# Who issues the fetches of the experts' first-layer weights in the routed FFN of a gated cross-attention block

## The chip, the cores and the metric

The kernel runs on one core of one Trainium2 chip. The metric is the device time of one execution in microseconds (us). The kernel before takes 317.39 us, the median of three runs (316.21 to 318.24).

## The reference, cut to what matters

4096 tokens (8 x 512) of width 256, float32. First a gated cross-attention, in which the 16 channels of a token's heads attend to one another, then a mixture of experts with top-1 routing:

```python
x = x + tanh(g_xattn[0]) * xattn(layernorm(x), ctx, Wq, Wk, Wv, Wo)
# ffn on xf = layernorm(x).reshape(4096, 256), E = 8 experts
idx = argmax(softmax(xf @ Wg + bg), axis=-1)
h   = gelu(einsum('th,ehi->tei', xf, W1) + b1)          # W1: 8 x 256 x 256
y   = einsum('tei,eih->teh', h, W2) + b2                # W2: 8 x 256 x 256
x   = x + tanh(g_ffn[0]) * take_along_axis(y, idx)      # one expert a token
```

## The kernel before, in words

**Two stages.** The first runs over 16 pairs of 128-token tiles: projections, scores, softmax, values, output projection, residual, gate logits. For each tile it works out each token's expert and its place, and scatters the rows (with mean, rstd and token number) to `routed_rows` in HBM, where each expert has a region. This stage ends at about 213 us of the trace.

**The expert stage** runs over 39 blocks (32 tiles + 8 experts - 1) of 128 routed rows, each block of one expert. Which rows and which expert a block has stands in the table `tab` in SBUF. So each fetch first loads an address or an expert number from `tab` into a register (`value_load`), then waits for its ring slot, then issues the DMA. Per block b, with ring slot q = b % 8 (`RING = 8`):

- SyncE (SP) fetches the block's rows, `xb[q]`, 134 KB, in `fetch` (L367 to L374). Before it may, it waits for `yf_done`, the end of block b - 8 on VectorE.
- The first-layer weights of the block's expert, `w1_sb[q]`, 257 KB, are fetched in `fetch_w1` (L315 to L319). SP does it for even q and for the first eight blocks. For odd q from block 9 on ScalarE does it (`act_fetches`, L321): in its slot b, behind the GELU of block b and the copy for block b + 2, it fetches w1 of block b + 3. Blocks 0 to 15 stand in the table's first part (`tab_done` 1), blocks 16 and up in its second (`tab_done` 2).
- VectorE normalizes (`norm_b`, L993): in its slot b the rows of block b + 3, and then it finishes block b - 1 (L1002, L1006, the last being `yf`).
- TensorE in its slot b does three things in a fixed order: layer 1 of block b (L557, 8 matmuls, waits for the copied transposes and for `w1_in[q]`), layer 2 of block b - 1 (L571, 4 matmuls), and the transposes of block b + 2 (L547, 2 matmuls). The order is written by hand.
- ScalarE in its slot b does the GELU of block b (L696), the copy of the transposes of block b + 2 (L703), and on even slots the fetch above.
- GpSimd stores the finished rows by an indirect DMA (L1244).

The second-layer weights of all experts stay in SBUF. Blocks 0 to 15 (`EARLY`) are written out one by one, with the end of the routing woven in; blocks 16 to 31 are two turns of a loop of eight blocks on each engine (`block_slots`, L268), with the block number in a register; blocks 32 to 38 are written out again. Each engine keeps its own order, and only semaphores tie them.

Of the kernel before, what the change touches and what calls it, by code (L numbers as in the profile page):

```python
# [32 lines left out]
RING = 8  # L33
OUT = 4
EARLY = 2 * RING
# [11 lines left out]
def wait(eng, sem, value):  # L47

    if isinstance(value, int) and value <= 0:
        return  # L50
    eng.wait_ge(sem, value)
# [27 lines left out]
def flamingo_block(nc, x, x_t, ctx_t, g_x, g_f, w_kv, w_qg, w_o, wo_t, bg, w1b, w2, b2, consts, out):  # L79
# [4 lines left out]
    blocks = tiles + E - 1  # L84
# [8 lines left out]
    with ExitStack() as stack:  # L93
# [6 lines left out]
        def sem(name):  # L100
            return stack.enter_context(nc.semaphore(name))
# [130 lines left out]
        tab_step, tab_done, turned = sem("tab_step"), sem("tab_done"), sem("turned")  # L232
# [34 lines left out]
        def block_slots(eng, slot, skew):  # L267
            with eng.Fori(EARLY // RING, blocks // RING) as turn:  # L268
                for q in range(RING):
                    slot(RING * turn + q, q, turn)  # L270
            for b in range(blocks - blocks % RING, blocks + skew):
                slot(b, b % RING, b // RING)
# [14 lines left out]
        def load_x(eng, n, i, count):  # L287
            wait(eng, x_in[i], count)
            eng.dma_start(x_sb[:, bass.ds(2 * n, 2), 0:D], x_v[:, bass.ds(2 * n, 2), :]).then_inc(x_in[i], 16)

        def load_ct(eng, n, i):
            wait(eng, kv_done, n - 1 if not isinstance(n, int) or n > 1 else 0)
            eng.dma_start(ct[i][:].rearrange("p a b c -> p (a b c)"),
                          ctx_t[bass.ds(n, 1)].rearrange("a p f -> p (a f)")).then_inc(ct_in[i], 16)

        def load_xt(eng, n, i):
            wait(eng, q_done, n - 1 if not isinstance(n, int) or n > 1 else 0)
            eng.dma_start(xt[i][:].rearrange("p a b c -> p (a b c)"),
                          x_t[bass.ds(n, 1)].rearrange("a p f -> p (a f)")).then_inc(xt_in[i], 16)

        def spread_k(eng, n, i, blocks_of):

            eng.wait_ge(yk_out, n + 1)
            for t in blocks_of:
                eng.dma_start(kb[i][H * t:H * t + H, t, :], y_k[i][H * t:H * t + H, :]).then_inc(kb_in[i], 16)

        def spread_v(eng, n, i, blocks_of):

            wait(eng, av_done, n - 1 if not isinstance(n, int) or n > 1 else 0)
            eng.wait_ge(yv_out, n + 1)  # L310
            for t in blocks_of:
                c, s = t // 2, t % 2
                eng.dma_start(vb[i][H * t:H * t + H, 4 * s + c, :], y_v[i][H * t:H * t + H, :]).then_inc(vb_in[i], 16)

        def fetch_w1(eng, b, q):  # L315

            ex = eng.value_load(tab[0:1, 1, bass.ds(b, 1)], min_val=0, max_val=E - 1)
            wait(eng, gelu_done, b - RING + 1)
            eng.dma_start(w1_sb[q][:], w1b[bass.ds(ex, 1)].rearrange("a p f -> p (a f)")).then_inc(w1_in[q], 16)  # L319

        def act_fetches(b, q):  # L321

            return q % 2 == 1 and not (isinstance(b, int) and b < RING)


        @block.sync
        def _(sp):
            def late_w2(e):
                sp.dma_start(w2_sb[:, bass.ds(e, 2)], w2[:, bass.ds(e, 2)]).then_inc(late_in, 16)

            def late_b2(e):
                sp.dma_start(b2_sb[:, bass.ds(e, 2), :].rearrange("p e d -> p (e d)"),
                             b2.rearrange("(e d) -> e d", d=D)[bass.ds(e, 2)].rearrange("e d -> (e d)").partition_broadcast(P)).then_inc(late_in, 16)
                sp.dma_start(rows.rearrange("(e r) w -> r e w", e=E)[0:P, bass.ds(e, 2)],
                             pad_row[:].unsqueeze(1).broadcast_to([P, 2, ROW])).then_inc(pad_in, 16)

            load_ct(sp, 0, 0)
            sp.dma_start(wkv[:, 1], w_kv[:, 1]).then_inc(wkv_in[1], 16)
            load_x(sp, 0, 0, 0)
            load_xt(sp, 0, 0)  # L340
            sp.dma_start(cst[:], consts).then_inc(cst_in, 16)
            load_xt(sp, 1, 1)
            sp.wait_ge(kb_clear[0], 1)
            spread_k(sp, 0, 0, range(4, T8))
            sp.wait_ge(vb_clear[0], 1)
            spread_v(sp, 0, 0, range(0, T8, 2))
            sp.wait_ge(kb_clear[1], 1)
            spread_k(sp, 1, 1, range(T8))
            sp.wait_ge(vb_clear[1], 1)
            spread_v(sp, 1, 1, range(T8))  # L350

            def slot(k, q):
                spread_k(sp, k + 2, q, range(T8))
                spread_v(sp, k + 2, q, range(T8))

            slot(0, 0)
            slot(1, 1)
            sp.wait_ge(consts_ok, 1)
            sp.wait_ge(wog_done, 1)
            with sp.Fori(1, E // 2 + 1) as turn:  # L360
                late_w2(2 * turn - 2)
                slot(2 * turn, 0)
                late_b2(2 * turn - 2)
                slot(2 * turn + 1, 1)
            for k in range(E + 2, pairs - 2):
                slot(k, k % 2)

            def fetch(b, q, turn):

                row = sp.value_load(tab[0:1, 0, bass.ds(b, 1)], min_val=0, max_val=(E - 1) * region + tokens)  # L370
                wait(sp, yf_done, b - RING + 1)
                sp.dma_start(xb[q][:], rows[bass.ds(row, P), :]).then_inc(xb_in[q], 16)
                if not act_fetches(b, q):
                    fetch_w1(sp, b, q)  # L374

            sp.wait_ge(tab_done, 1)
            sp.wait_ge(routed, 32 * (last_pair - 2))
            for b in range(EARLY):
                fetch(b, b % RING, b // RING)
            sp.wait_ge(tab_done, 2)  # L380
            sp.wait_ge(routed, 32 * pairs)
            sp.wait_ge(pad_in, 16 * E // 2)
            block_slots(sp, fetch, 0)
            for i in range(OUT):
                sp.wait_ge(stored[i], 16 * ((blocks + OUT - 1 - i) // OUT))
# [228 lines left out]
        def _(act):  # L614
# [64 lines left out]
            def expert_slot(b, q, turn):  # L679
                i = q % 2  # L680
                known = isinstance(b, int)
                if not known or b < blocks:
                    gelu(b, q)
                if not known or b + 2 < blocks:
                    copy_xbt(b + 2, i)
                ahead = 3
                if (not known or b + ahead < blocks) and act_fetches(b + ahead, (q + ahead) % RING):
                    fetch_w1(act, b + ahead, (q + ahead) % RING)

            def gelu(b, q):  # L690

                i = q % 2
                act.wait_ge(h_done, b + 1)
                wait(act, y_done, b - 1)
                for ic in range(KC):
                    last = act.activation(ht[i][:, ic, :], h_ps[i][:, ic * P:(ic + 1) * P], ACT.Gelu,  # L696
                                          bias=w1_sb[q][:, KC * D + ic:KC * D + ic + 1])
                last.then_inc(gelu_done, 1)

            def copy_xbt(b, i):  # L700
                act.wait_ge(xbt_done, b + 1)
                wait(act, h_done, b - 1)
                act.copy(xbt[i][:].rearrange("p a b -> p (a b)"), x_t_ps[i]).then_inc(xbt_out, 1)  # L703
# [5 lines left out]
            gelu(0, 0)  # L709
            copy_ot(last_pair)  # L710
            copy_xbt(2, 0)
            act.wait_ge(tab_done, 1)
            for b in range(1, EARLY):
                if b == EARLY - 3:
                    act.wait_ge(tab_done, 2)
                expert_slot(b, b % RING, b // RING)
            block_slots(act, expert_slot, 0)


# [591 lines left out]
```

## Time and profile before

| | us |
|---|---|
| median of 3 runs | 317.39 (316.21 to 318.24) |
| profiled execution, its own time | 320.28 |
| its span | 318.3 |
| TensorE busy | 287.7 (90%) |
| VectorE busy | 230.0 (72%) |
| ScalarE busy | 84.1 (26%) |
| GpSimd busy | 123.3 (39%) |
| mean granted TensorE clock | 0.982 |
| expert stage: layer 1 of block 1 to the last matmul | 220.9 to 308 |

The profiled execution took 2.9 us more than the median of the runs; 2.0 us of its time lie around its span. Issuing a DMA does not count as busy time, so SyncE has no line in the table; its issues stand in the timeline with their start and length. Matmuls of one engine overlap a little in the timeline, since their ends are modelled.

### The profile page before, as it was taken

To read this page: it belongs to the slowest core of one execution; us is meant where nothing else is said; L and a number is where in the kernel's file an instruction comes from. 1 tells how busy PE (TensorE), PEld (TensorE's weight loads), DVE (VectorE), ACT (ScalarE), POOL (GpSimd) and SP (SyncE) were. 2 spreads that over 40 slices of the span, in tenths; PEclk is the share of its full clock that TensorE was granted. 3 is DMA by queue.
4 is the path that set the end of the run, shared out by engine and by line. 5 is a ranking of instruction groups with operands and counts; after the bars stand their busy time and mean duration, and the time that the engine had idled before them with its cause. 6 is when DMAs were issued, how large, how long until landed. Compare 5 with 4: busy or idle time off the path is not lost.

```text
span 318.3 us, 10091 instructions
## 1 busy us (share of the span) xinstructions
PE 287.7 (90%) x3173; PEld 219.7 (69%) x3174; DVE 230.0 (72%) x810; ACT 84.1 (26%) x219; POOL 123.3 (39%) x125
## 2 busy tenths in 40 slices
PE   8989999999899999999999997687889998899870
PEld 7557767577577676776776775466778787889760
DVE  7558678797788888798887977867786664655550
ACT  1011320321312302303213213123434444454420
POOL 8502022442423523524424433432364444344441
PEclk9999999999999999999999999979999999999995
DMA  8575346466465565564455123277467887677610
GB/s 266 171 192 151 93 111 189 102 211 197 129 203 153 167 206 136 184 204 109 130 152 150 46 69 84 80 197 194 147 191 231 233 258 215 194 241 231 190 52 0
DMA packets 35482, 51.40 MB, mean 161 GB/s; under 512 B 8189, under 2 KB 18558, under 8 KB 35456
## 3 DMA queue, kind: packets, MB, share of 16 engines
q1 hardware_dynamic: 20240, 25.69, 30.7%
q10 hardware_dynamic: 11808, 16.81, 16.8%
q0 software_dynamic: 3408, 8.59, 7.6%
q8 instruction: 12, 0.20, 0.3%
q14 instruction: 14, 0.11, 0.1%
HBM read 32.99 MB, written 10.60 MB: 137 GB/s over the span
## 4 chain that ended last, share of the span: by engine, by line
PE 59%; issue 10%; DVE 10%; DMA 7%; ACTq 4%; POOL 3%; ACT 2%; another core or an unknown queue 1%; DVEq 1%; POOLq 0%
PE ps_pr L393 11%; PE ps_qo L401 11%; PE ps_av L439 5%; PE ps_tr L557 5%; PE ps_so L557 5%; PE ps_to L571 5%; PE ps_av L571 5%; PE ps_so L419 4%; DMA routed_rows<-sb_xs,sb_pos_i 4%; DMA sb_x<-x_in 3%; PE ps_pr L547 2%; POOL sb_cn L279 2%; PE ps_av L512 2%; PE ps_tr L428 1%; DVE sb_om L794 1%
## 5 line engine op out<-in xcount | busy, mean ns | idle before, releaser
L393 PE MATMUL ps_pr<-sb_wkv,sb_ct 128*128 128x512 f32 x128 | 63.0, 616 | 0.5 <-DVE sb_y_v L749 0.5
L279 POOL TENSOR_TENSOR sb_cn<-sb_om,sb_rt 128x512 f32<-128x512 f32 x15 | 19.3, 1287 | 68.5 <-DVE sb_om L794 68.5
L627 ACT ACTIVATE sb_pe_x<-sb_pe_x 128x512 f32<-128x512 f32 x16 | 10.1, 631 | 124.6 <-DVE sb_pe_x L770 108.2
L1213 POOL DMA_INDIRECT routed_rows<-sb_xs,sb_pos_i x32 | 32.2, 1006 | 21.0 <-DVE sb_pos_i L885 10.5
L393 PEld LDWEIGHTS ps_pr<-sb_wkv,sb_ct 128*128 128x128 f32 x128 | 22.3, 191 | 20.0 <-issue 19.8
L401 PE MATMUL ps_qo<-sb_wog,sb_ot 128*128 128x264 f32 x128 | 32.9, 402 | 1.3 <-ACT sb_q_n L622 1.1
L439 PE MATMUL ps_av<-sb_vb,sb_at 128*32 128x128 f32 x1024 | 32.6, 274 | 0.9 <-issue 0.9
L401 PEld LDWEIGHTS ps_qo<-sb_wog,sb_ot 128*128 128x128 f32 x128 | 25.2, 199 | 11.4 <-issue 7.3
L439 PEld LDWEIGHTS ps_av<-sb_vb,sb_at 128*32 128x32 f32 x1024 | 27.4, 110 | 7.1 <-issue 7.1
L419 PE MATMUL ps_so<-sb_kb,sb_y_q 128*32 128x128 f32 x1024 | 31.1, 273 | 0.5 <-DVE sb_y_q L755 0.5
L401 PE MATMUL ps_qo<-sb_wqg_c,sb_xt 128*128 128x264 f32 x128 | 31.1, 386 | 0.0
L1244 POOL DMA_INDIRECT out_rows<-sb_yf,sb_tok_i x20 | 19.7, 983 | 29.4 <-DVE sb_yf L1006 27.2
L419 PEld LDWEIGHTS ps_so<-sb_kb,sb_y_q 128*32 128x32 f32 x1024 | 28.0, 110 | 1.9 <-issue 1.4
L401 PEld LDWEIGHTS ps_qo<-sb_wqg_c,sb_xt 128*128 128x128 f32 x128 | 23.1, 190 | 3.6 <-DVE sb_wqg_c L1108 0.2
L1244 POOL DMA_INDIRECT out_rows<-sb_q_n,sb_tok_i x19 | 18.6, 980 | 17.2 <-issue 11.0
L557 PE MATMUL ps_tr<-sb_ct,sb_w 128*128 128x128 f32 x152 | 20.7, 279 | 4.1 <-ACT sb_ct L703 3.0
L1202 POOL TENSOR_TENSOR sb_rstd<-sb_ve,sb_neg_half 128x2 f32<-128x2 f32 x16 | 11.5, 716 | 33.1 <-ACT sb_q_n L622 18.2
L557 PEld LDWEIGHTS ps_tr<-sb_ct,sb_w 128*128 128x128 f32 x152 | 18.5, 191 | 5.8 <-ACT sb_ct L703 3.8
L1002 DVE TENSOR_TENSOR sb_yo<-ps_av,sb_b 128x256 f32<-128x256 f32 x20 | 8.5, 425 | 18.6 <-PE ps_av L571 12.5
L557 PE MATMUL ps_so<-sb_ct,sb_w 128*128 128x128 f32 x160 | 21.3, 276 | 0.1
L571 PE MATMUL ps_av<-sb_w,sb_ht 128*128 x80 | 21.3, 388 | 0.0
L571 PE MATMUL ps_to<-sb_w,sb_ht 128*128 x76 | 20.0, 385 | 1.3 <-ACT sb_ht L696 1.2
(129 smaller groups left out, 490.1 us busy)
## 6 DMA issues: line engine op xcount, KB each, us to landing
sb_w<-w_in_ SPq DMA_DIRECT2D x24, 257.0 KB, 3.2
sb_xb<-routed_rows SPq DMA_DIRECT2D x39, 134.0 KB
sb_kb<-sb_y_k SPq DMA_DIRECT2D x124, 32.0 KB
sb_vb<-sb_y_v SPq DMA_DIRECT2D x124, 32.0 KB
sb_w<-w_in_ ACTq DMA_DIRECT2D x15, 257.0 KB, 3.4
sb_ct<-ctx_in ACTq DMA_DIRECT2D x15, 256.0 KB, 3.2
sb_x<-x_in ACTq DMA_DIRECT2D x15, 256.0 KB, 5.6
sb_xt<-xt_in_ ACTq DMA_DIRECT2D x14, 256.0 KB, 4.1
```

The lines of the kernel that those rows point to most:

```text
L279: eng.tensor_tensor(cn[:].rearrange("p u h i -> p h u i"), om[:].rearrange("p h (u i) -> p h u i", u=2), rt[:].rearrange("p (u i) -> p u i ...
L393: last = pe.matmul(pr[:, s * 512:(s + 1) * 512], lhsT=ct[i][:, kc, s, :], rhs=wkv[:, kc, :], start=(kc == 0), stop=(kc == KC - 1))
L401: last = pe.matmul(dst[:, s * 512:s * 512 + DE], lhsT=src[:, kc, s, :], rhs=w[:, kc, :], start=(kc == 0), stop=(kc == KC - 1))
L419: last = pe.matmul(so[32 * q:32 * q + 32, r * P:(r + 1) * P], lhsT=y_q[:, 4 * q + r, u:u + 2, :].rearrange("p a b -> p (a b)"), rhs=kb[i][ ...
L439: last = pe.matmul(av[32 * q:32 * q + 32, r * P:(r + 1) * P], lhsT=at[:, 4 * r + q, u:u + 2, :].rearrange("p a b -> p (a b)"), rhs=vb[i][: ...
L557: last = pe.matmul(h_ps[i][:, ic * P:(ic + 1) * P], lhsT=w1_sb[q][:, kc * D + ic * P:kc * D + (ic + 1) * P], rhs=xbt[i][:, kc, :], start=( ...
L571: last = pe.matmul(y_ps[i], lhsT=ht[i][:, ic, :], rhs=w2_sb[:, bass.ds(ex, 1), ic, :].rearrange("p a d -> p (a d)"), start=(ic == 0), stop ...
L627: act.activation(pe_x[:], pe_x[:], ACT.Exp, scale=float(H) ** -0.5).then_inc(exp_done, 1)
L1002: dve.tensor_tensor(yo[i][:], y_ps[i], b2_sb[:, bass.ds(ex, 1), :].rearrange("p a d -> p (a d)"), ALU.add).then_inc(yb_done, 1)
L1202: pool.tensor_tensor(rstd[:], ve[:], neg_half[:], ALU.pow).then_inc(ln_pow, 1)
L1213: pool.indirect_dma_start(rows, bass.IndirectOffsetOnAxis(ap=pos_i[:, s:s + 1], axis=0), xs[:, s, :], None).then_inc(routed, 16)
L1244: pool.indirect_dma_start(out, bass.IndirectOffsetOnAxis(ap=tok_i[j][:, 0:1], axis=0), yf[j], None, bounds_check=tokens - 1, oob_is_err=Fa ...
```

## The change

All first-layer weights are fetched by SP, each right behind the rows of its block. ScalarE fetches none, and its two waits for the table, which only its fetches needed, go. Nothing else moves: the ring, the slots and the work of the other engines are the same.

```diff
-        def act_fetches(b, q):
-
-            return q % 2 == 1 and not (isinstance(b, int) and b < RING)
...
                 sp.dma_start(xb[q][:], rows[bass.ds(row, P), :]).then_inc(xb_in[q], 16)
-                if not act_fetches(b, q):
-                    fetch_w1(sp, b, q)
+                fetch_w1(sp, b, q)
...
                     copy_xbt(b + 2, i)
-                ahead = 3
-                if (not known or b + ahead < blocks) and act_fetches(b + ahead, (q + ahead) % RING):
-                    fetch_w1(act, b + ahead, (q + ahead) % RING)
...
             copy_xbt(2, 0)
-            act.wait_ge(tab_done, 1)
             for b in range(1, EARLY):
-                if b == EARLY - 3:
-                    act.wait_ge(tab_done, 2)
                 expert_slot(b, b % RING, b // RING)
```

On SyncE, inside the loop over blocks 16 to 31, at the first odd block of a turn. Before, the rows of block q = 1 (`sb_xb`) are followed at once by the rows of block q = 2 and then by the weights of q = 2 (`sb_w_2`):

```order
L372 DMA sb_xb<-routed_rows 128x268
L370 ISA
L370 TENSOR_LOAD sb_tab
L370 ISA x2
L51 REGISTER_ALU
L372 ISA [waits yf_done]
L372 DMA sb_xb<-routed_rows 128x268
L317 ISA
L317 TENSOR_LOAD sb_tab
L317 ISA x2
L319 ISA [waits gelu_done]
L319 DMA sb_w_2<-w_in_ 128x514
```

In the changed kernel the same place on SyncE reads:

```order
L367 DMA sb_xb<-routed_rows 128x268
L317 ISA
L317 TENSOR_LOAD sb_tab
L317 ISA x2
L319 ISA [waits gelu_done]
L319 DMA sb_w_1<-w_in_ 128x514
L365 ISA
L365 TENSOR_LOAD sb_tab
L365 ISA x2
L51 REGISTER_ALU
L367 ISA [waits yf_done]
L367 DMA sb_xb<-routed_rows 128x268
```

The table load, the register work, the wait and the DMA of an odd block's weights now stand between the rows of that block and the rows of the next; 15 such pieces in all (blocks 9, 11, ... 37).

On ScalarE, at the start of a loop turn (slot q = 0), before:

```order
L696 ACTIVATE sb_ht<-ps_so,sb_w_0 128x128
L701 REGISTER_ALU
L703 COPY sb_ct<-ps_pr 128x256 [waits h_done,xbt_done]
L317 ISA
L317 TENSOR_LOAD sb_tab
L317 ISA x2
L51 REGISTER_ALU
L319 ISA [waits gelu_done]
L319 DMA sb_w_3<-w_in_ 128x514
L693 REGISTER_ALU
L696 ACTIVATE sb_ht<-ps_tr,sb_w_1 128x128 [waits y_done,h_done]
```

and in the changed kernel:

```order
L687 ACTIVATE sb_ht<-ps_so,sb_w_0 128x128
L692 REGISTER_ALU
L694 COPY sb_ct<-ps_pr 128x256 [waits h_done,xbt_done]
L684 REGISTER_ALU
L687 ACTIVATE sb_ht<-ps_tr,sb_w_1 128x128 [waits y_done,h_done]
```

The fetch for three blocks ahead is gone from between the copy and the next GELU.

## Rows read from the trace of the kernel before

**Rows 1.** Timeline of TensorE: start, length, what; idle time before it in brackets
```profile
237.97 1.06 PE L557 MATMUL ps_so<-sb_ct,sb_w 128*128 128x128 f32 x8
...
256.31 1.06 PE L557 MATMUL ps_so<-sb_ct,sb_w 128*128 128x128 f32 x8
...
258.88 1.13 PE L557 MATMUL ps_tr<-sb_ct,sb_w 128*128 128x128 f32 x8 [0.43 <-ACT sb_ct L703]
...
268.30 1.13 PE L557 MATMUL ps_tr<-sb_ct,sb_w 128*128 128x128 f32 x8 [1.11 <-ACT sb_ct L703]
...
305.63 1.05 PE L557 MATMUL ps_so<-sb_ct,sb_w 128*128 128x128 f32 x8
```
**Rows 2.** The chain that ended last: start, length, what
```profile
254.50 0.89 PE ps_tr L557 x8
255.39 0.86 PE ps_av L571 x4
256.26 0.22 PE ps_pr L547 x2
...
304.04 0.89 PE ps_tr L557 x8
...
308.57 0.47 DVE sb_yf L1006
```
**Rows 3.** Waits of TensorE from 245 to 306 us: total, times, longest
```profile
PE ps_tr L557 <- ACT sb_ct L703: 3.0, 4, 1.1
...
PE ps_tr L557 <- issue: 1.1, 3, 0.4
```
**Rows 4.** Timeline of ScalarE's queue: the DMA issues for blocks 17, 21 and 25
```profile
255.21 0.34 ACTq L319 DMA_DIRECT2D sb_w<-w_in_  x1
...
264.11 0.34 ACTq L319 DMA_DIRECT2D sb_w<-w_in_  x1
...
273.88 0.34 ACTq L319 DMA_DIRECT2D sb_w<-w_in_  x1
```
**Rows 5.** ScalarE's issues of L319 alone: from issue to landing
```profile
DMA to landing us min/median/max: 3.2/3.4/4.2
```
**Rows 6.** Timeline of SyncE, written-out blocks: rows and weights of blocks 6, 7
```profile
218.09 0.33 SPq L372 DMA_DIRECT2D sb_xb<-routed_rows  x1
219.18 0.33 SPq L319 DMA_DIRECT2D sb_w<-w_in_  x1
220.27 0.33 SPq L372 DMA_DIRECT2D sb_xb<-routed_rows  x1
221.35 0.33 SPq L319 DMA_DIRECT2D sb_w<-w_in_  x1
```
**Rows 7.** Timeline of SyncE from 245 to 262 us: blocks 16 to 23
```profile
246.71 0.33 SPq L372 DMA_DIRECT2D sb_xb<-routed_rows  x1
...
253.73 1.57 SPq L372 DMA_DIRECT2D sb_xb<-routed_rows  x2
256.15 0.33 SPq L319 DMA_DIRECT2D sb_w<-w_in_  x1
```
**Rows 8.** The same from 262 us on, and from 224 to 250 us
```profile
262.83 0.34 SPq L372 DMA_DIRECT2D sb_xb<-routed_rows  x1
...
242.64 0.17 SPq L319 DMA_DIRECT2D sb_w<-w_in_  x1
244.91 2.14 SPq L372 DMA_DIRECT2D sb_xb<-routed_rows  x2
```
**Rows 9.** Waits of SyncE's queue over the whole span
```profile
SPq L372 <- DVE sb_yf L1006: 7.7, 5, 3.1
...
SPq L372 <- DVE sb_q_n L1006: 3.3, 3, 1.2
```
**Rows 10.** VectorE's line L993: min, median, max in ns
```profile
L993 DVE TENSOR_SCALAR sb_ct<-sb_xb x39: 397/408/512, 213.5 to 300.1; 128x256 f32<-128x256 f32 x39
```
**Rows 11.** Busy time by stretch: us, PE, PEld, DVE, ACT, POOL, granted clock, DMA
```profile
204.70:208.10 3.40, 0.98 (x7) 0.50 (x5) 2.78 (x14) 2.39 (x4) 0.72 (x1) 1.00 0.58 155
208.10:211.50 3.40, 3.25 (x9) 2.60 (x10) 1.18 (x10) 0.79 (x2) 0.91 (x1) 0.51 0.62 141
265.00:268.40 3.40, 2.29 (x17) 1.93 (x16) 2.56 (x8) 1.54 (x5) 1.96 (x2) 1.00 0.83 239
```

## The prediction

> **What bounds the kernel now.** The change touches only the expert stage, so I read TensorE's timeline there, then the chain that ended last, then what TensorE waits for, then who issues what it waits for.
>
> An undisturbed slot of TensorE in the chain is 0.89 + 0.86 + 0.22 = 1.97 us long [rows 2], 1.98 with the rounding: 254.50 to 256.48: layer 1, layer 2, transposes. That is the floor for a block. From layer 1 of block 8 to layer 1 of block 38 there are 30 slots, and they take 305.63 - 237.97 = 67.7 us [rows 1]. At the floor they would take 29 x 1.98 + 1.76 = 59.2 us (the last slot has no transposes). So 8.5 us are to be had in this stretch, and that is the most that any mending of the fetches can bring there.
>
> Where are they? TensorE stands before layer 1 in seven slots from 245 us on, 4.1 us in all [rows 3], and after each stand the slot is some tenths longer (1.13 against 1.06 for the matmuls) [rows 1]. The blocks with a stand are 17, 21 and other odd ones. The profile puts some of the waits down to ScalarE's copy, but the copy of that block had been made two slots earlier. ScalarE issued the weights of block 17 at 255.21 and of block 21 at 264.11 [rows 4]; with 3.2 to 4.2 us to landing [rows 5] they are there at 258.4 to 259.4 and 267.3 to 268.3, and layer 1 starts at 258.88 and 268.30 [rows 1]. So the stands are **late weights**: ScalarE issues them behind its GELU and copy, about two slots (4 us) before layer 1 wants them, which is hardly more than their landing time. The change removes this.
>
> **The change part by part.**
>
> *ScalarE.* 15 table loads, register steps and DMA issues leave it. It is no bound: it is 26% busy over the span, and what it gives back is the stands above, counted already. Its two waits for the table go; the table's second half is there long before block 16. Nothing on the path, cost 0.
>
> *SyncE.* It gets 15 more pieces. The price of a piece is read where SP waits for nothing. In written-out code it is one issue every 1.09 us, rows or weights alike: 218.09, 219.18, 220.27, 221.35 [rows 6]. In the loop, two issues of rows span 1.57 us of which the last 0.33 is the second issue itself: 1.24 us for rows; from their end at 255.30 to the end of the next weights' issue at 256.48: 1.18 us for weights [rows 7]. So a block costs SP 2.42 us in the loop and 2.18 outside, against TensorE's 1.98. Before, the mean over a pair in the loop was (2 x 1.24 + 1.18) / 2 = 1.83 us, under the floor. **SP becomes the slowest engine of the stage.**
>
> *What covers it.* In blocks 8 to 14 SP waits for yf: 11.0 us in 8 waits, some of them there [rows 9], so the pieces of blocks 9, 11 and 13 (3 x 1.09) fall into idle time: 0. From block 15 on the cover is gone, since SP issues the rows of 15 as soon as it can. After that the ring does not hold SP back: a block is finished about 5.0 us after its layer 1 starts (308.57 + 0.47 against 304.04 for block 37 [rows 2]) and layer 1 starts some 5.6 to 6 us after the rows are issued (below), together under 11 us, while SP needs 8 x 2.42 = 19.4 us for a round.
>
> *The lead.* The rows of block 16 go out at 246.71 [rows 7] and its layer 1 starts at 256.31 [rows 1]: 9.6 us of lead. What is needed: landing of the rows, then 0.41 for the normalization [rows 10], then TensorE's transposes 0.22, layer 1 of the block before 0.89 and layer 2 of the one before that 0.87 [rows 2]. For the rows' landing the trace has no figure; the weights, twice as large, need 3.2 to 4.2 [rows 5], and I take 3.2, near the low end for the smaller transfer. Sum 5.6 us. The lead is 4 us longer than that, and 2.42 - 1.98 = 0.44 us is eaten a block, so it would be gone after nine blocks; and as TensorE itself is sooner without the stands, earlier still. After that each block starts when SP lets it.
>
> *The sum, as SP's clock.*
> - rows of block 16: 246.71 + 1.09 (weights of block 15) = 247.8
> - 16 blocks in the loop: 16 x 2.42 = 38.7
> - SP's slow spots: from 246.71 to 262.83 [rows 7, 8] one turn takes 16.1, where 8 x 1.24 + 4 x 1.18 = 14.6 were due, so 1.5 us a turn are lost; for two turns 3.0
> - rows of block 32: 289.5; then six rows and six weights at 1.09: 13.1, so rows of block 38 at 302.6
> - layer 1 of block 38: 5.6 later, 308.2
>
> Before it was 305.63. The tail behind it is unchanged. **+2.6 us.** The 8.5 us that the late weights cost are given back by SP, and a little more.
>
> *Bounds.* Between the weights of block 14 and the rows of 16 SP takes 3.9 us where two or so issues were due (242.64 + 0.17 to 246.71 [rows 7, 8]), so 1.6 are a slow spot there too; if that and the 3.0 of the loop vanish, and the rows land in 2.9, the sum is -2.3. If the loss goes with the number of issues (1.5 for 12, so 3.9 for 32), with 1.0 more at the entry, 0.7 in the last blocks, and a landing of 3.8, it is +5.8. I take the middle case since slow spots of a turn are measured once and nothing says that ScalarE's issues cause them.
>
> *A rule against the trace.* The rows show issue time of 2.42 us a block as more than the matmuls it feeds [rows 2, 7]. The Trainium skill, "DMA: Bandwidth & Descriptors", section "Issuing engines are not separate DMA queues", says that starting DMAs on several engines only saves the sequencer's time, "which is usually small relative to the DMA itself". By it the sum would be the stands given back alone. Here no row shows it small: 1.18 us stand beside 3.2 of the DMA.
>
> **The rivals.**
>
> *A, SP keeps up.* Then only the stands go: 4.1 us of waiting at the least [rows 3] and 8.5 us, all that lies over the floor, at the most; with the slower restarts some 7. Time 317.4 - 7 = 310.4. For it: TensorE's stands are real and end with the landing. Against it: it needs under 1.98 us a block from SP, and no pair of neighbouring issues in the rows gives less than 2.18. The rule above speaks for it. 8%.
>
> *B, slower beyond doubt.* SP's slow spots grow with its code: two instructions then take some tenths more each, at the entry to the loop and in each turn. The price is the upper bound, +3.2 to +5.8 us; its middle gives 322. It decides from the point where the rows of block 38 go out later than 303.2 us (305.63 + 3.2 - 5.6). For it: the forecast is at 302.6 already. 38%.
>
> *C, the clock.* With SP as the bound TensorE has 1.98 of 2.42 us busy, 82%. The granted clock fell to half (0.51) behind a stretch with 0.98 us busy of 3.40, and it stayed at 1.00 in one with 2.29 of 3.40, 67% [rows 11]. So I do not expect a fall; one would cost about as much again as the matmuls in it, some 3 us. 3%, within B's range.
>
> *D, the change does not do what it says.* Excluded by the order of the instructions: 15 fetches left ScalarE and stand on SyncE. 0%.
>
> **How the numbers follow.** The profiled execution would take 320.28 + 2.6 = 322.9. The median of the runs shown lies 2.9 lower, so the forecast is 317.39 + 2.6 = 320.0. Forecast with its neighbours (-3.2 to +3.2): 46%. About 1% (3.2 us) is what a measurement of this kernel tells from no change. The bounds give 315.1 to 323.2; A and what lies beyond the upper bound are left out, under 20% together. Faster by over 1%: A and a lucky end of the lower bound, 13%. Slower by over 1%: B with C, 41%, as the forecast is only 0.6 us below that line. Same: 46%.
>
> **What would show it.** In the changed kernel's profile SP's issues are 1.2 us apart without a pause from about 250 us to the end, with no wait for yf from block 16 on; rows of block 32 go out near 289.5 and of block 38 near 302.6. TensorE's idle time moves from before layer 1 to before the transposes (L541 there), released by the normalization, about 0.4 us in every block from some block between 16 and 20. ScalarE has no DMA issue there and is never waited for. It is wrong if TensorE runs at 1.98 us a block for long behind block 20 (A), if SP's pieces shrink once ScalarE issues nothing, or if layer 1 waits for weights still.

## The result

The changed kernel takes 322.25 us, the median of four runs (321.14 to 324.67), beside 317.81 us for the kernel before: 1.0154 times as long, 95% interval 1.0107 to 1.0202. Two more comparisons of the same two kernels, described with the experiments, gave 1.0031 (0.9984 to 1.0078) and 1.0109 (1.0062 to 1.0156). Two of the three intervals lie above 1 and the third takes it in. So it is slower, by about 1%, some 3 us; the forecast was 320.0 us, +2.6.

The profiled execution took 321.91 us, its span is 320.0 us.

**The same points as before in TensorE's timeline** (start, length, what, idle before): layer 1 of blocks 8, 16, 21 and 38, with the transposes ahead of that of block 21. The line numbers of the changed kernel are lower, by 6 on TensorE and 12 on VectorE: L551 is the old L557, L541 the old L547, L981 the old L993.

```profile
235.79 1.06 PE L551 MATMUL ps_so<-sb_ct,sb_w 128*128 128x128 f32 x8
...
253.10 1.06 PE L551 MATMUL ps_so<-sb_ct,sb_w 128*128 128x128 f32 x8
...
267.08 0.44 PE L541 MATMUL ps_pr<-sb_cst,sb_ct 128*128 128x128 f32 x2 [1.18 <-issue]
267.36 1.06 PE L551 MATMUL ps_tr<-sb_ct,sb_w 128*128 128x128 f32 x8
...
307.27 1.05 PE L551 MATMUL ps_so<-sb_ct,sb_w 128*128 128x128 f32 x8
```

From block 8 to block 38 the stage takes 307.27 - 235.79 = 71.5 us, against 67.7 [rows 1]: 3.8 us more. The stretches around it are the same length within the scatter: 12.7 us follow layer 1 of block 38 in both, and block 8 starts 2.2 us sooner here, which the other traces show to be scatter (it starts between 233.9 and 239.6 in all eleven). The stand is no longer before layer 1 but before the transposes.

**Waits of TensorE from 245 to 309 us**, to be held against [rows 3]:

```profile
PE ps_pr L541 <- issue: 4.3, 4, 1.2
PE ps_pr L541 <- DVE sb_ct L981: 2.1, 4, 1.0
PE ps_to L565 <- DVE sb_yo L990: 0.5, 1, 0.5
PE ps_so L551 <- issue: 0.3, 1, 0.3
...
PE ps_so L551 <- ACT sb_ct L694: 0.2, 1, 0.2
```

The waits before layer 1 have shrunk from 4.1 us to 0.5, and 6.4 us have come before the transposes, which need VectorE's normalized rows. Why VectorE is late stands in the groups of instructions from 245 us to the end (busy us, mean ns, then idle time before them and its releaser); first the kernel before, then the changed one:

```profile
L993 DVE TENSOR_SCALAR sb_ct<-sb_xb 128x256 f32<-128x256 f32 x25 | 10.2, 409 | 0.1
```

```profile
L981 DVE TENSOR_SCALAR sb_ct<-sb_xb 128x256 f32<-128x256 f32 x25 | 11.1, 443 | 14.6 <-DMA sb_xb<-routed_rows 14.2 <-issue 0.4
```

VectorE, which stood 0.1 us before this step, now waits 14.2 us for the rows' landing. And what the rows wait for is SP.

**SP's timeline** at the rows of block 16, in the middle of the loop (blocks 22 and 23), at the rows of block 24, where the second turn of the loop begins, at those of block 32 and at the last two issues, answering [rows 6 to 8]:

```profile
246.04 0.33 SPq L367 DMA_DIRECT2D sb_xb<-routed_rows  x1
247.49 0.09 SPq L319 DMA_DIRECT2D sb_w<-w_in_  x1
...
262.60 0.33 SPq L367 DMA_DIRECT2D sb_xb<-routed_rows  x1
263.78 0.33 SPq L319 DMA_DIRECT2D sb_w<-w_in_  x1
264.95 0.33 SPq L367 DMA_DIRECT2D sb_xb<-routed_rows  x1
266.11 0.33 SPq L319 DMA_DIRECT2D sb_w<-w_in_  x1
267.75 0.34 SPq L367 DMA_DIRECT2D sb_xb<-routed_rows  x1
...
287.62 0.33 SPq L367 DMA_DIRECT2D sb_xb<-routed_rows  x1
...
300.76 0.34 SPq L367 DMA_DIRECT2D sb_xb<-routed_rows  x1
302.18 0.34 SPq L319 DMA_DIRECT2D sb_w<-w_in_  x1
```

Here SP issues about every 1.2 us, now and then some tenths later (266.11 to 267.75) and once by 1.7, and from 245 us on it never waits for `yf`. Rows of block 16 to rows of block 32 take 41.6 us, and to those of block 38 another 13.1. Its waits for `yf` over the whole span, 11.0 us in 8 waits before [rows 9], 4.4 of them behind 263 us, are 3.1 us in 3:

```profile
SPq L367 <- DVE sb_yf L994: 2.1, 2, 1.9
SPq L367 <- DVE sb_q_n L994: 1.0, 1, 1.0
```

### The profile page after: what moved, and what is told of

The parts are those of the page before. It is cut to its first block, busy times and chain, and to the rows that moved or that the text cites. A ratio compares the mean times of both kernels' runs of the same rounds, so it can differ in the third digit from the quotient of the medians.

```text
span 320.0 us, 10085 instructions
## 1 busy us (share of the span) xinstructions
PE 287.4 (90%) x3173; PEld 218.8 (68%) x3174; DVE 232.0 (73%) x810; ACT 84.0 (26%) x218; POOL 123.9 (39%) x125
## 4 chain that ended last, share of the span: by engine, by line
PE 53%; issue 13%; DVE 11%; SPq 9%; DMA 4%; ACTq 2%; POOL 2%; DVEq 2%; ACT 1%; POOLq 0%
PE ps_qo L395 15%; PE ps_pr L387 15%; PE ps_av L433 8%; PE ps_so L413 7%; DMA sb_xb<-routed_rows 4%; PE ps_tr L422 3%; SPq L367 2%; SPq L317 2%; SPq L365 2%; SPq L319 2%; PE ps_to L446 2%; PE ps_av L506 2%; POOL out_rows L1232 1%; DVEq L987 1%; DVE sb_st L796 1%
## 5 line engine op out<-in xcount | busy, mean ns | idle before, releaser
L387 PEld LDWEIGHTS ps_pr<-sb_wkv,sb_ct 128*128 128x128 f32 x128 | 22.2, 191 | 19.7 <-issue 19.5
L981 DVE TENSOR_SCALAR sb_ct<-sb_xb 128x256 f32<-128x256 f32 x39 | 17.0, 437 | 14.6 <-DMA sb_xb<-routed_rows 14.2
L694 ACT COPY sb_ct<-ps_pr 128x256 f32<-128x256 f32 x39 | 14.4, 373 | 37.3 <-PE ps_pr L541 28.4
L541 PE MATMUL ps_pr<-sb_cst,sb_ct 128*128 128x128 f32 x78 | 15.6, 283 | 7.5 <-issue 4.5
L551 PE MATMUL ps_so<-sb_ct,sb_w 128*128 128x128 f32 x160 | 21.4, 277 | 0.7 <-ACT sb_ct L694 0.4
```

Of the source, the lines that this page charges most:

```text
L387: last = pe.matmul(pr[:, s * 512:(s + 1) * 512], lhsT=ct[i][:, kc, s, :], rhs=wkv[:, kc, :], start=(kc == 0), stop=(kc == KC - 1))
L541: last = pe.transpose(x_t_ps[i][:, kc * P:(kc + 1) * P], xbn[i][:, kc * P:(kc + 1) * P], ident)
L551: last = pe.matmul(h_ps[i][:, ic * P:(ic + 1) * P], lhsT=w1_sb[q][:, kc * D + ic * P:kc * D + (ic + 1) * P], rhs=xbt[i][:, kc, :], start=( ...
L981: dve.tensor_scalar(xbn[i][:], xb[q][:, 0:D], xb[q][:, MEAN:MEAN + 1], xb[q][:, RSTD:RSTD + 1], ALU.subtract, ALU.mult).then_inc(xbn_done, 1)
```

## The experiments

Below, "the stage" is the time from the start of layer 1 of block 8 to that of block 38, read in the trace as above: 67.7 us before, 71.5 us changed.

### Weights fetched without reading the expert (e1)

```diff
-            ex = eng.value_load(tab[0:1, 1, bass.ds(b, 1)], min_val=0, max_val=E - 1)
+            ex = q
```

> The changed kernel, but each weights fetch takes a fixed expert (the slot number) instead of reading it from the table; so blocks get the wrong first-layer weights, and the transfers are as many, as large and on the same queue. Issue-rate theory: a weights piece falls from 1.18 to about 0.53 us (no table load, no register steps), a block costs SP 1.24 + 0.53 = 1.77 us, under TensorE's 1.98, so SP no longer bounds and the late weights are gone too: 308 to 313 us, some 7 below the kernel before. Shared-queue theory (rows land late since they stand behind the weights in SP's own queue, whatever SP's pace): nothing gained, 320 to 324 us.

This kernel leaves out the choice of the expert, so it is a probe of the time alone. Measured: 309.85 us, ratio to the kernel before 0.9756 (0.9714 to 0.9798). The stage takes 59.4 us. SP's timeline shows what a weights piece costs without the table load and its register steps. It starts 0.39 us behind the rows and ends 0.48 us behind their end, where it was 1.18:

```profile
263.18 0.34 SPq L367 DMA_DIRECT2D sb_xb<-routed_rows  x1
263.57 0.43 SPq L319 DMA_DIRECT2D sb_w<-w_in_  x1
265.24 0.33 SPq L367 DMA_DIRECT2D sb_xb<-routed_rows  x1
265.63 0.43 SPq L319 DMA_DIRECT2D sb_w<-w_in_  x1
```

The transfers, their sizes and their queue are those of the changed kernel, and 12 us are gone: SP's instructions around the DMA had cost them. What the shared queue costs does not reach the time. The rows even take longer to land here (median 3.4 us from issue, 2.7 in the changed kernel's second trace, e7), but they are issued 10.5 us before layer 1 of block 38. Two rows of SP are 2.06 us apart here, more than it needs, because it waits for the ring again.

### ScalarE fetches five blocks ahead (e2)

```diff
-                ahead = 3
+                ahead = 5
...
-                if b == EARLY - 3:
+                if b == EARLY - 5:
                     act.wait_ge(tab_done, 2)
```

> The kernel before, with ScalarE fetching the odd blocks' weights five blocks ahead instead of three. Late-weights theory: TensorE's stands before layer 1 go, SP stays at 1.83 us a block: 308 to 312 us. If the stands came from ScalarE's own delay (its issues in front of the GELU and the copy) and not from the landing: 316 to 318 us, no change.

Measured: 310.43 us, ratio 0.977 (0.9738 to 0.9803). This one computes all that the kernel before does and beats both. TensorE's timeline, at blocks 8 and 38 and over two blocks between:

```profile
236.34 1.06 PE L557 MATMUL ps_so<-sb_ct,sb_w 128*128 128x128 f32 x8
...
264.42 1.06 PE L557 MATMUL ps_so<-sb_ct,sb_w 128*128 128x128 f32 x8
265.31 1.03 PE L571 MATMUL ps_to<-sb_w,sb_ht 128*128 x4
266.18 0.38 PE L547 MATMUL ps_pr<-sb_cst,sb_ct 128*128 128x128 f32 x2
266.40 1.06 PE L557 MATMUL ps_tr<-sb_ct,sb_w 128*128 128x128 f32 x8
...
295.84 1.05 PE L557 MATMUL ps_so<-sb_ct,sb_w 128*128 128x128 f32 x8
```

The stage takes 59.5 us, where the prediction had 59.2 as the floor, and a slot is 1.98 us here and on the mean of the 30. So the stands before layer 1 were the late weights, and ScalarE's own work in front of its GELU (still there) costs nothing.

### The same, with idle table loads on SP (e3)

```diff
                 if not act_fetches(b, q):
                     fetch_w1(sp, b, q)
+                else:
+                    for _ in range(2):
+                        sp.value_load(tab[0:1, 1, bass.ds(b, 1)], min_val=0, max_val=E - 1)
```

> As the five-ahead kernel, but SP also does two idle table loads (about 0.65 us each) for every odd block from 9 on, in the place where the changed kernel has its weights fetch; no transfer is moved. Issue-rate theory: SP needs 1.24 + (1.18 + 1.30) / 2 = 2.48 us a block as in the changed kernel, 320 to 325 us. Shared-queue theory: as the five-ahead kernel, 308 to 312 us.

Measured: 318.99 us, ratio 1.0045 (1.0008 to 1.0083), a little under the expected 320 to 325. No transfer differs from e2, yet 8.6 us are lost. The stage takes 68.0 us (238.77 to 306.73), and VectorE waits for rows as in the changed kernel:

```profile
L996 DVE TENSOR_SCALAR sb_ct<-sb_xb 128x256 f32<-128x256 f32 x26 | 11.5, 444 | 13.8 <-DMA sb_xb<-routed_rows 13.7
```

With e1 this crosses the two theories: many transfers on SP's queue and few instructions are fast; few transfers and many instructions are slow.

### The changed kernel with one more idle load a block (e4)

```diff
                 fetch_w1(sp, b, q)
+                if not (isinstance(b, int) and b < RING):
+                    sp.value_load(tab[0:1, 1, bass.ds(b, 1)], min_val=0, max_val=E - 1)
```

> The changed kernel with one more idle table load on SP behind each block's weights fetch from block 8 on. Issue-rate theory: 0.65 us more for each of the 24 blocks 15 to 38 that SP paces, some 15 us: 333 to 341 us. Shared-queue theory: 320 to 325 us.

Measured: 330.64 us in one execution, below the expected 333 to 341, but 8 to 10 us over the changed kernel's three medians. SP's timeline in the last blocks:

```profile
300.17 0.34 SPq L367 DMA_DIRECT2D sb_xb<-routed_rows  x1
301.28 0.33 SPq L319 DMA_DIRECT2D sb_w<-w_in_  x1
302.91 0.33 SPq L367 DMA_DIRECT2D sb_xb<-routed_rows  x1
304.00 0.33 SPq L319 DMA_DIRECT2D sb_w<-w_in_  x1
```

From rows to weights it is 1.09 to 1.11 us still, from weights over the idle load to rows 1.63: a load costs 0.54, not the 0.65 that the expectation had. 24 of them make 13.0 us; the stage takes 82.0 us (233.92 to 315.89), which is 10.5 over the changed kernel's first trace and 12.6 over the mean of its three (69.4, below). The direction and the mechanism hold, the price was set too high.

### A dose between (e5), and seven blocks ahead (e6)

e5 starts from e2:

```diff
-            return q % 2 == 1 and not (isinstance(b, int) and b < RING)
+            return q % 4 == 3 and not (isinstance(b, int) and b < RING)
```

> A dose between the five-ahead kernel and the changed one: ScalarE fetches the weights of every fourth block only (slots 3 and 7, five blocks ahead), SP those of the other three. Issue-rate theory: SP needs 1.24 + 0.75 x 1.18 = 2.13 us a block, with its slow spots 2.25; from layer 1 of block 8 to that of block 38 some 64 us, between the 59.5 of the five-ahead kernel and the 71.5 of the changed one, so 313 to 317 us. If the change's cost came from something that only starts when ScalarE fetches nothing at all: 309 to 311 us.

Measured: 314.9 us, ratio 0.9845 (0.9779 to 0.991). The stage takes 62.0 us (239.61 to 301.57), two less than expected, but between the others. The time lies in the expected range. The cost grows with SP's share and does not wait until ScalarE fetches nothing.

e6 is e2 with 7 for 5:

```diff
-                ahead = 5
+                ahead = 7
```

> The kernel before with ScalarE's fetch seven blocks ahead. Late-weights theory: at five blocks ahead TensorE is at its floor already, so nothing more: 309 to 312 us. If the landing time still cost something at five: 1 us or more below the five-ahead kernel.

Measured: 312.2 us, 0.2 above the expected range, ratio 0.9777 (0.9702 to 0.9853), the same ratio as e2. The stage takes 59.3 us (238.79 to 298.07). Once the weights are in time, more distance brings nothing.

### Both kernels again (e7, e8, e9)

> The changed kernel again, beside the two others on one chip. All theories: 320 to 325 us, 71 to 72 us from layer 1 of block 8 to that of block 38, and 9 to 13 us above the seven-ahead kernel.

Measured: 320.36 us, ratio 1.0031 (0.9984 to 1.0078). It is 8 us above e6, a little less than expected, and the stage takes 68.6 us (238.52 to 307.10), not 71 to 72: the expectation missed there.

> The kernel before once more, for a second trace of its expert stage. Issue-rate theory: SP is not what paces it, so the late weights cost what they did: 66 to 69 us from layer 1 of block 8 to that of block 38 (67.7 before), whatever SP's slow spots do in blocks 8 to 15. Span 315 to 321 us.

Measured: 320.31 us in one execution, span 318.4; the stage takes 67.0 us (238.63 to 305.67), as expected.

> The changed kernel a third time, with more rounds, since the two comparisons so far gave 1.5% and 0.3%. Issue-rate theory: from SP's rows of block 16 to those of block 38 again 54.7 us (54.7 in both traces), and the stretch before it, blocks 8 to 16, is where the traces differ (22.7 and 20.4 us). Ratio to the kernel before 1.003 to 1.015.

Measured: 320.39 us, ratio 1.0109 (1.0062 to 1.0156). The stage takes 68.2 us (236.02 to 304.20). Rows of blocks 16, 24, 32 and 38 in SP's timelines, first of e7, then of e9:

```profile
246.39 0.33 SPq L367 DMA_DIRECT2D sb_xb<-routed_rows  x1
...
267.84 0.34 SPq L367 DMA_DIRECT2D sb_xb<-routed_rows  x1
...
287.31 0.33 SPq L367 DMA_DIRECT2D sb_xb<-routed_rows  x1
...
301.08 0.34 SPq L367 DMA_DIRECT2D sb_xb<-routed_rows  x1
```

```profile
244.31 0.33 SPq L367 DMA_DIRECT2D sb_xb<-routed_rows  x1
...
265.02 0.34 SPq L367 DMA_DIRECT2D sb_xb<-routed_rows  x1
...
284.49 0.33 SPq L367 DMA_DIRECT2D sb_xb<-routed_rows  x1
...
298.75 0.34 SPq L367 DMA_DIRECT2D sb_xb<-routed_rows  x1
```

Where SP paces the stage, the three traces agree: 54.7, 54.7 and 54.4 us. They differ at both ends of that stretch, as the table shows (us, from starts in the timelines):

| | layer 1 of block 8 to rows of 16 | rows of 16 to rows of 38 | rows of 38 to its layer 1 | sum |
|---|---|---|---|---|
| forecast | 9.8 | 54.8 | 5.6 | 70.2 |
| changed, first trace | 10.3 | 54.7 | 6.5 | 71.5 |
| changed, e7 | 7.9 | 54.7 | 6.0 | 68.6 |
| changed, e9 | 8.3 | 54.4 | 5.5 | 68.2 |

**All stages beside SP's price for a block** (1.24 for rows, 1.18 for weights, 0.54 for an idle load, in the loop):

| kernel | SP, us a block | stage, us |
|---|---|---|
| e2, e6 (five, seven ahead) | 1.83 | 59.5, 59.3 |
| e1 (no table load for the weights) | 1.24 + 0.48 = 1.72 | 59.4 |
| e5 (three in four on SP) | 2.13 | 62.0 |
| e3 (two idle loads for odd blocks) | 1.24 + 1.18 / 2 + 0.54 = 2.37 | 68.0 |
| changed | 2.42 | 71.5, 68.6, 68.2 |
| e4 (one idle load more) | 2.96 | 82.0 |

Under TensorE's 1.98 us the stage is at its floor, above it it grows with SP's price. The kernel before, at 1.83 with its late weights, has 67.7 and 67.0.

## Why the prediction was right

**The floor and the late weights.** Both held. 59.2 us was the floor by the chain; e1, e2 and e6 have 59.3 to 59.5. The 8.5 us over it were laid to the weights that ScalarE fetched late; e2 takes away 8.2 of them by fetching earlier and nothing else.

**ScalarE at no cost.** Held: with its fetches (e2) and without them (e1) the stage is the same within 0.1 us.

**SP's clock.** 16 blocks at 2.42 us and 3.0 us of slow spots were to take 41.7 us from rows of 16 to rows of 32, and took 41.6, 40.9 and 40.2 in the three traces; the last twelve issues were to take 13.1, and took 13.1, 13.8 and 14.3. Together 54.8 against 54.4 to 54.7. Of the slow spots only the sum came out, and that is partly luck: the prediction read one turn of the loop (1.5 us lost) and doubled it. In the changed kernel the first turn takes 21.7, 21.5 and 20.7 us where 19.4 are due (2.3, 2.1 and 1.4 lost), the second 19.9, 19.5 and 19.5 (0.5, 0.1 and 0.1 lost). Even the 1.5 was one trace's: in e8 the kernel before loses 0.5 in that turn (16.3 us, 1.2 of them waits for `yf`, where 14.6 are due). Why the first turn is the slow one no run shows. e3 shows that it is the instructions that cost, without any transfer moved.

**The cover.** The weights of blocks 9, 11 and 13 were to fall into SP's waits for `yf`, those of 15 not. The term (9.8 us from layer 1 of block 8 to rows of 16) was 10.3 in the first trace and 7.9 and 8.3 in the others; in the first SP also had a slow spot between the rows of blocks 14 and 15, 4.1 us apart (240.07 to 244.18) where 2.2 were due. So 9.8 was on the high side, and one execution could not tell that. The same stretch in the kernel before is 8.7 us in its first trace and 6.7 in e8. The mean grows from 7.7 to 8.8 with the change, which is the one piece of 1.09 that the prediction added; what was high was the start it added it to.

**The last latency.** 5.6 us from rows to layer 1 was 6.5, 6.0 and 5.5, so the estimate was low by 0.4 on average. The landing was taken too long, not too short: 3.2, where the medians are 2.7 (e7) and 2.8 (e9), from 2.1 to 4.6. What the term left out is that the rows of block 38 find TensorE still busy with the blocks before. With the entry 1.0 too high, SP's stretch 0.2 too high and this 0.4 too low, the forecast of the stage is 0.8 over the mean; part of the error cancels.

**Size.** The forecast change of the stage, +2.5 (70.2 against 67.7), compares with +2.1 between the means of the traces (69.4 and 67.35), and the +2.6 us of time with 4.9, 1.0 and 3.5 us in the three comparisons (their ratios times the time before). The result that stands first has the largest of them; it lies in the range and, at 1.5%, on the side of "slower by over 1%", which had 41%, while the likeliest case had 46%.

**The rivals.** A, SP keeps up, is out: nothing in SP's price fell when ScalarE issued nothing. What A hoped for is real (e2 has 310.4, as A had), but it needs SP's price under 1.98. B gave the right sign of the first result by the wrong mechanism: slow spots did not grow with SP's code by anything that stands out of their scatter, and the rows of block 38 went out at 298.8 to 301.1 us, never behind B's 303.2. In e4, with more instructions, 16 blocks in the loop take 49.6 us where 16 x 2.96 = 47.4 are due, a loss of 2.2 as in the changed kernel's 2.9, 2.2 and 1.5. With 24 issues in place of 32, e2 and e6 lose 1.6 each (30.9 us where 29.3 are due), which may be somewhat less or the same. C did not happen: the granted clock is 1.00 from 245 to 308 us with TensorE 55.6 of 63.0 us busy (88%, where the prediction had 82%).

```profile
245.00:308.00 63.00, 55.61 (x369) 47.87 (x369) 35.71 (x105) 25.85 (x80) 25.65 (x26) 1.00 0.72 197
```

**The rule that was weighed.** The Trainium skill, "DMA: Bandwidth & Descriptors", section "Issuing engines are not separate DMA queues", holds in its first half as far as the traces go: in e2 weights issued by SP land after a median of 3.6 us, those issued by ScalarE after 3.5. Its second half, that the saved issue time is usually small beside the DMA, does not hold here: a fetch of weights costs SP 1.18 us beside a landing of 3.1 us (e7), and that made SP the bound. The issuing instruction itself is 0.33 us of the 1.18, and the table load with its register steps makes up more than half: without them it is 0.48 (e1).

**Signs that came otherwise.** ScalarE was never to be waited for; TensorE's layer 1 waits 0.2 us for its copy, once. And TensorE was to stand about 0.4 us in every block. It stands 0.3 to 1.2 us before the transposes in about every third block and not at all in others, 6.4 us in all (5.0 in e7, 3.9 in e9). Part of the lumps can be read from the landings. The rows of block 21 are issued at 260.19 and normalized 2.3 us later, those of block 22 at 262.60 and 3.9 us later, at 266.51:

```profile
262.53 0.42 DVE L981 TENSOR_SCALAR sb_ct<-sb_xb 128x256 f32<-128x256 f32 x1 [0.35 <-DMA sb_xb<-routed_rows]
266.51 0.52 DVE L981 TENSOR_SCALAR sb_ct<-sb_xb 128x256 f32<-128x256 f32 x1 [1.46 <-DMA sb_xb<-routed_rows]
```

The stand of 1.18 us shown above is the one before the transposes of block 22. The blocks right behind have had that time to land, and TensorE runs through them without a stand. Why some rows take longer to land was not settled.

## What to carry to other kernels

Count what a queue issues per round of the loop, with the register loads and address steps that each dynamic DMA needs, and compare it with the bound engine's round: here 2.42 us against 1.98 turned an engine without any "busy" time into the bound, and without the table load for the weights it would have stayed under (e1, 1.72). When a transfer is late, first issue it earlier on the engine that has it (one distance changed, -2.3%), before moving it to another queue. A wait that moves from one instruction to another (layer 1 to the transposes) names the new bound only when it is followed back, here over VectorE and the rows' landing to SP.

## What the runs showed of the hardware

- A `value_load` from a table in SBUF costs SP's queue 0.54 us (1.63 against 1.09 between issues in e4). Without it two DMAs go out 0.39 us apart (e1), where the second issue takes 0.43 us and not 0.33.
- SP has slow spots in which an issue comes 0.1 to 2 us later than its neighbours, in the changed kernel some 1.5 to 2.9 us for 16 blocks, most of it in the first turn of the loop. They were there with and without ScalarE's issues (1.6 in e2 and e6). With more instructions in e4 they were no longer (2.2); whether they grow a little with the number of issues, their scatter hides. Their cause stays open.
- The slow spots are of two kinds. In the first trace of each of the two kernels there are runs in which SP takes 0.7 us for each small step (a register MOVE, 0.03 us otherwise, takes up to 0.71), as between the rows of blocks 16 and 17 (246.04 and 250.46) of the changed kernel. The nine later traces, three of the same two kernels among them, have none of these (their longest MOVE is 0.04); there single table loads (0.27 us otherwise) take up to 0.77 and single DMA issues (0.33 otherwise) up to 1.25. So the runs of slow steps belong to the execution and not to the kernel.
- One comparison of this kernel is only good to about 1%: three comparisons of the same two kernels gave 1.0154, 1.0031 and 1.0109, while the stretch that SP paces was 54.4 to 54.7 us each time.
